# Conv tower: the low fp16 parts of every layer made by GpSimd alone, DVE keeping the high parts and the statistics

## The chip, the core and the metric

The kernel runs on one core of one Trainium2 chip. The metric is the device time of one execution in microseconds. The core has TensorE (PE; matmuls, weight loads shown apart as PEld), VectorE (DVE), ScalarE (ACT), GpSimd (POOL) and SyncE (SP, which issues transfers); each works through its own instructions in order and waits on semaphores for the others.

## What is computed

An audio tower in fp32: six convolution layers, one attention layer with 12 heads, one layer of 8 experts with top-1 routing, for a batch of 4 sequences of 120,000 samples. The change concerns the convolutions only:

```python
CONV_LAYERS = [(128, 10, 5), (128, 3, 2), (128, 3, 2), (128, 3, 2), (128, 3, 2), (128, 2, 2)]
NUM_GROUPS = 32

def _block(x, cw, cb, gw, gb, stride):
    y = lax.conv_general_dilated(x, cw, (stride,), 'VALID', dimension_numbers=('NCH', 'OIH', 'NCH'))
    y = y + cb[None, :, None]
    B, C, T = y.shape
    yg = y.reshape(B, NUM_GROUPS, C // NUM_GROUPS * T)
    mu = yg.mean(axis=-1, keepdims=True)
    var = yg.var(axis=-1, keepdims=True)
    yn = ((yg - mu) * lax.rsqrt(var + EPS)).reshape(B, C, T)
    yn = yn * gw[None, :, None] + gb[None, :, None]
    return jax.nn.gelu(yn)
...
h = tower(x)
h = h + attention(layernorm(h))
h = h + experts(layernorm(h))
```

The group normalisation of a layer needs the mean and variance over the whole sequence of the layer's output, so a layer's activations can't be finished before its last convolution is.

## The kernel before

**Two fp16 parts.** TensorE multiplies in fp16, and each fp32 activation is kept as two fp16 parts: the high part is the value cast to fp16, the low part is the value less the high part. A convolution is summed from three products per tap: high weights and low weights with the high part, high weights with the low part. In a group of up to 9 matmuls (3 taps) the 6 with the high part come first, and the 3 with the low part wait for it. All parts lie in one large SBUF tile, `arena`, whose rows have 126 columns; 8 rows are 1008 elements per partition.

**A pass of the tower.** The tower runs once per sequence, four passes in all, and nothing of a pass overlaps the next pass's tower. In a pass:

1. Layer 0's output is made in 24 pieces of 8 rows (`conv0` jobs, three per block j). TensorE makes a piece in PSUM, ScalarE normalises it into one of 4 staging buffers (line 991), DVE casts it to the high part (1178), and GpSimd or DVE makes the low part (794 or 1181). A staging buffer is written again when high and low part of the piece four earlier are done. Layer 1's convolutions, 96 rows in jobs of two cuts of 4 rows, are interleaved: a cut reads rows from the three pieces of a block, so it waits for the parts of a block's last piece (2, 5, 8, ...). Their outputs go through ScalarE (972) to fp32 rows, and DVE takes their statistics (`bn_stats`, line 1315, 1311 and 1312).
2. When the last statistics are in, a short chain (aggregate 1093, TensorE's group average 1703, GpSimd's power 769, DVE 1116) gives scale and bias. ScalarE normalises layer 1's 96 rows in 13 chunks of 5, 4, ten times 8, and 7 rows (903), DVE casts each chunk, one of the two engines makes the low part, and TensorE begins layer 2's 48 rows as the chunks come in. After the last cast DVE copies one row of the high and one of the low part to the end of the buffer, the halo (1171, 1172), which the last convolution job of the next layer waits for. Only then, in DVE's order, come the statistics of layer 2's rows.
3. The same for layer 2 (7 chunks), layer 3 (4 chunks) and layer 4 (2 chunks, no halo). Layer 5's output goes into the attention.

**Who makes a low part** is decided by `low_engine`: of layer 0, DVE makes every third piece (2, 5, 8, ...) and GpSimd the others; of layers 1 to 4, DVE the even chunks (0, 2, 4, ...) and GpSimd the odd ones. DVE makes its low part right behind the cast of the same chunk. GpSimd makes each when `hi_done` says that its cast is done (`low_parts`, line 794), in the chunks' order. TensorE and ScalarE wait for the low parts by the two counters `lo_dve` and `lo_pool`. Attention, experts and the work between passes use neither of the two lines.

Of the kernel before, what the change touches and what calls it, by code (L numbers as in the profile page):

```python
# [50 lines left out]
ACT_ENGINE, DVE_ENGINE = "act", "dve"  # L51
# [92 lines left out]
SETUP, TOWER, PAIR, LAST_PAIR, POST, MOE = range(6)  # L144
# [47 lines left out]


def low_engine(layer, piece):
    if layer == 0:
        return DVE_ENGINE if piece % 3 == 2 else "pool"
    return "pool" if piece % 2 else DVE_ENGINE

# [9 lines left out]
    "affine_ready": (1, CONV_LAYERS - 1, 0, 0, 1),  # L210
    "norm_done": (0, sum(len(c) for c in NORM_CHUNKS.values()), 0, 0, 0),
    "hi_done": (0, len(SPLITS), 0, 0, 0),
    "lo_dve": (0, sum(low_engine(*u) == DVE_ENGINE for u in SPLITS), 0, 0, 0),
    "lo_pool": (0, sum(low_engine(*u) == "pool" for u in SPLITS), 0, 0, 0),
    "halo_done": (0, 4, 0, 0, 0),
    "xn_ready": (0, 1, 0, 0, 1),
# [103 lines left out]
def audio_tower(nc, ins, out):  # L320
# [8 lines left out]
    with ctx:  # L329
# [543 lines left out]
        def _(act):  # L873
# [87 lines left out]
            with act.Fori(0, BATCH) as b:  # L961
                layer = 0
                for g, n, kind, args in jobs_of(TOWER):
                    if kind == "conv":
                        if args[0] > 1 and args[1] == 0:
                            normalise(args[0] - 1, b)
                        layer, r, cut = args
                        wait(act, "ps_full", TOWER, n + 1, b)
                        rows = cut[0]
                        dst = ys[layer][:, r * PITCH:(r + sum(cut)) * PITCH]  # L970
                        src = slot(g).rearrange("p (k n) -> p k n", k=2)[:, 0:len(cut), 0:rows * PITCH]
                        a.activation(dst.rearrange("p (k n) -> p k n", k=len(cut)), src, ACT.Identity,  # L972
                                     scale=1.0 / WSCALE).then_inc(S["act_freed"], 1)
                    elif kind == "conv0":
                        j, i = args
                        if args == (0, 0):
                            wait(act, "affine_ready", TOWER, 0, b)

                            wait(act, "scratch_stored", TOWER, 0, b)
                        wait(act, "ps_full", TOWER, n + 1, b)  # L980
                        piece = 3 * j + i
                        if piece >= STAGES:

                            had_it = (0, piece - STAGES)
                            wait(act, "hi_done", TOWER, SPLITS.index(had_it) + 1, b)
                            if low_engine(*had_it) == DVE_ENGINE:
                                wait(act, "lo_dve", TOWER, lows(DVE_ENGINE, had_it), b)
                            else:
                                wait(act, "lo_pool", TOWER, lows("pool", had_it), b)
                        src = slot(g).rearrange("p (m n) -> p m n", m=2)[:, :, 0:4 * PITCH]  # L990
                        a.activation(stage[:, piece % STAGES, :].rearrange("p (m n) -> p m n", m=2), src,  # L991
                                     ACT.Gelu_apprx_tanh,
                                     bias=affine[:, 1:2], scale=affine[:, 0:1]).then_inc(S["act_freed"], 1)
                    elif kind in ("q", "k", "v", "s"):
                        attention_job(TOWER, g, n, kind, args, b)
                    else:
                        assert kind == "xtr"
                        if layer == 5:
                            normalise(5, b)
                            layer = None  # L1000
                        wait(act, "ps_full", TOWER, n + 1, b)
                        a.activation(xt_parts[:, args[0], :], bank(g, 0).bitcast(fp16)[:, 0:TOK], ACT.Copy
                                     ).then_inc(S["act_freed"], 1)
                with act.Fori(0, PAIRS - 1) as pr:
                    for g, n, kind, args in jobs_of(PAIR):
                        attention_job(PAIR, g, n, kind, args, b, pr)
                for g, n, kind, args in jobs_of(LAST_PAIR):
                    attention_job(LAST_PAIR, g, n, kind, args, b)
                for g, n, kind, args in jobs_of(POST):
                    wait(act, "ps_full", POST, n + 1, b)  # L1010
                    a.activation(xnt1[0:D1, 0:TOK], slot(g)[0:D1, 0:TOK], ACT.Copy).then_inc(S["act_freed"], 1)
# [22 lines left out]
        def _(dve):  # L1034
# [139 lines left out]
            def split(unit, b):  # L1174

                src, high, low = split_views(*unit)
                n = SPLITS.index(unit) + 1
                v.tensor_copy(high, src).then_inc(S["hi_done"], 1)  # L1178
                if low_engine(*unit) == DVE_ENGINE:
                    dve.wait_ge(S["hi_done"], at("hi_done", TOWER, n, b))  # L1180
                    v.tensor_tensor(low, src, high, ALU.subtract).then_inc(S["lo_dve"], 1)  # L1181

            def wait_split(unit, b):
                wait(dve, "hi_done", TOWER, SPLITS.index(unit) + 1, b)
                for engine, name in ((DVE_ENGINE, "lo_dve"), ("pool", "lo_pool")):
                    if lows(engine, unit):
                        wait(dve, name, TOWER, lows(engine, unit), b)

            def attention_job(phase, n, kind, args, b, pr=None):
                g = slot_of(phase, n)  # L1190
# [283 lines left out]
        def _(pe):  # L1474
# [213 lines left out]
            with pe.Fori(0, BATCH) as b:  # L1688
                for n, (kind, args, who) in enumerate(JOBS[TOWER]):
# [11 lines left out]
                    elif kind == "group":  # L1701
                        wait(pe, "channel_stats", TOWER, args[0], b)
                        last = t.matmul(bank(g, 0)[:, 0:2], group_avg[:, :], ms[:, :], start=True, stop=True)
                    elif kind == "conv":
                        layer, r, cut = args
                        taps = 2 if layer == 5 else 3
                        parts = [a.rearrange("p (r c) -> p r c", c=PITCH) for a in hs[layer - 1]]

                        terms = [(tap, w, 0) for tap in range(taps) for w in (0, 1)]
                        terms += [(tap, 0, 1) for tap in range(taps)]  # L1710
                        for k, c in enumerate(cut):
                            need = 2 * (r + c) - 2 + taps - 1
                            if need >= ROWS[layer - 1]:
                                wait(pe, "halo_done", TOWER, layer, b)
                                need = ROWS[layer - 1] - 1
                            unit = split_unit_of(layer - 1, need)
                            wait(pe, "hi_done", TOWER, SPLITS.index(unit) + 1, b)
                            for tap, w, x in terms:
                                if (tap, w, x) == (0, 0, 1):
                                    for engine, name in ((DVE_ENGINE, "lo_dve"), ("pool", "lo_pool")):  # L1720
                                        wait(pe, name, TOWER, lows(engine, unit), b)
                                f = 2 * r + tap
                                last = t.matmul(bank(g, k)[:, 0:c * PITCH].rearrange("p (r c) -> p r c", c=PITCH),  # L1723
                                                cwt[layer][:, w, tap, :], parts[x][:, f:f + 2 * c - 1:2, :],
                                                start=(tap, w, x) == terms[0], stop=(tap, w, x) == terms[-1])
                            r += c
                    elif kind == "embed":
                        if args[0] == 0:
                            wait(pe, "norm_done", TOWER, COUNTS["norm_done"][1], b)
                        tiles = range(4) if args[0] == 0 else range(4, TT)  # L1730
                        for q, i in enumerate(tiles):
                            m = tile_rows(i)
                            last = t.matmul(bank(g, q // 2)[0:m, (q % 2) * D:(q % 2 + 1) * D],
                                            h5t[:, 128 * i:128 * i + m], pwt[:, :], start=True, stop=True)
                    else:
                        assert kind == "xtr"
                        if args[0] == 0:
                            wait(pe, "xn_ready", TOWER, 1, b)
                        for i in range(TT):
                            m = tile_rows(i)  # L1740
                            last = t.transpose(bank(g, 0).bitcast(fp16)[:, 128 * i:128 * i + m],
                                               xn_parts[0:m, i, args[0], :], ident_h[0:m, 0:m])
# [142 lines left out]
```

## Time and profile before

| | |
|---|---|
| median of 3 runs | 1911.61 us |
| lowest, highest | 1901.88, 1912.4 us |
| span of the profiled execution | 1912.2 us |
| busy share of the span: PE, DVE, ACT, POOL | 80%, 58%, 40%, 31% |
| passes of the tower, from the first cast of layer 0 to the last cast of layer 4 | 39.80 to 184.15, 440.53 to 586.29, 842.56 to 988.86, 1245.38 to 1391.67 us |

The busy shares are averages over the tower, the attention and the experts. Durations count from an instruction's start, which can lie before the moment at which it gets what it needs, so an instruction can be long because it is held. Successive instructions of one engine overlap a little at their ends: two casts of 0.67 us take 1.27 in a row.

### The profile page before, as it was taken

The numbers are of one execution on the slowest core, as the hardware profiler recorded it, in microseconds if no ns is written. First come the engines' busy times: TensorE is split into PE (matmuls) and PEld (weight loads), VectorE is DVE, ScalarE is ACT, GpSimd is POOL, SyncE is SP. The second block draws the span as 40 slices with busy tenths as digits, with TensorE's granted clock in tenths as the row PEclk, the third lists the DMA queues.
The fourth block names the chain that finished last, engine by engine and source line by source line (L and its number), as shares of the span: only waits on it lengthen the run. The fifth ranks groups of instructions, "written<-read, shape, count | busy, mean of one in ns | idle before, by whom it ended". The sixth has DMA issues, their size and how long they took to land.

```text
span 1912.2 us, 33119 instructions
## 1 busy us (share of the span) xinstructions
PE 1539.1 (80%) x10013; PEld 1020.7 (53%) x10014; DVE 1109.6 (58%) x2520; ACT 757.7 (40%) x1456; POOL 600.9 (31%) x502
## 2 busy tenths in 40 slices
PE   6975699998865899889657999898659999339997
PEld 4332476783333666763334666833336667327775
DVE  5986455568884555669864555598845555302221
ACT  2643344425542444425533444165324443002221
POOL 3732133305431333236322333064213331421111
PEclk6987799998986999979877999989869999659999
DMA  4200121210000221110001222100014332621110
GB/s 125 80 1 1 34 57 41 56 34 12 1 1 1 65 56 41 33 36 1 1 1 40 53 48 51 30 11 1 1 28 105 89 73 66 199 69 46 48 47 20
DMA packets 105852, 81.31 MB, mean 43 GB/s; under 512 B 57842, under 2 KB 96267, under 8 KB 105747
## 3 DMA queue, kind: packets, MB, share of 16 engines
q1 hardware_dynamic: 99988, 70.65, 14.6%
q0 software_dynamic: 5760, 9.36, 1.6%
q8 instruction: 54, 0.88, 0.2%
q14 instruction: 50, 0.41, 0.1%
HBM read 34.66 MB, written 18.38 MB: 28 GB/s over the span
## 4 chain that ended last, share of the span: by engine, by line
issue 40%; PE 35%; POOL 15%; DVE 5%; SPq 2%; DMA 2%; ACT 1%; POOLq 0%; DVEq 0%; ACTq 0%
POOL arena L794 10%; PE ps L1676 8%; PE ps L1618 6%; PE ps L1650 4%; PE ps L1662 3%; PE ps L1830 3%; PE ps L1625 2%; PE ps L1810 2%; PE ps L1811 2%; DVE arena L1212 2%; DVE smax L1203 2%; POOL slot_scratch L848 1%; PE ps L1818 1%; SPq L552 1%; PE ps L1831 1%
## 5 line engine op out<-in xcount | busy, mean ns | idle before, releaser
L1723 PE MATMUL ps<-arena,cwt 128*128 128x504 f16 (+2 forms) x1776 | 409.8, 392 | 85.3 <-DVE arena L1178 59.9
L1723 PEld LDWEIGHTS ps<-arena,cwt 128*128 128x128 f16 x1776 | 179.4, 105 | 305.9 <-DVE arena L1178 66.2
L794 POOL TENSOR_TENSOR arena<-arena 128x1008 f16<-128x1008 f32 (+2 forms) x112 | 255.6, 2292 | 196.6 <-DVE arena L1178 196.6
L1676 PE MATMUL ps<-arena 128*128 128x64 f32 (+2 forms) x2016 | 261.2, 270 | 22.9 <-DVE arena L1212 22.9
L1203 DVE TENSOR_REDUCE smax<-ps 128x1 f32<-128x128 f32 (+5 forms) x288 | 177.2, 615 | 172.1 <-PE ps L1653 172.1
L1676 PEld LDWEIGHTS ps<-arena 128*128 128x128 f32 (+2 forms) x2016 | 242.3, 189 | 44.2 <-issue 28.5
L1212 DVE COPY arena<-ps 128x512 f32<-128x512 f32 (+4 forms) x288 | 157.4, 546 | 83.7 <-PE ps L1662 83.6
L1181 DVE TENSOR_TENSOR arena<-arena 128x1008 f16<-128x1008 f32 (+2 forms) x88 | 200.3, 2276 | 3.0
L917 ACT ACTIVATE arena<-ps,nmax 128x128 f32<-128x128 f32 (+5 forms) x288 | 180.6, 627 | 53.5 <-DVE nmax L1204 50.7
L1178 DVE CAST arena<-arena 128x1008 f16<-128x1008 f32 (+4 forms) x200 | 176.9, 914 | 32.6 <-ACT arena L903 16.1
L1650 PE MATMUL ps<-arena 128*128 128x512 f16 (+6 forms) x780 | 163.7, 313 | 28.9 <-ACT arena L957 16.3
L1662 PE MATMUL ps<-ident,arena 128*128 128x128 f32 (+2 forms) x1008 | 168.0, 284 | 12.1 <-ACT arena L957 5.7
L972 ACT ACTIVATE arena<-ps 128x1008 f32<-128x1008 f32 (+1 forms) x112 | 96.1, 865 | 186.3 <-PE ps L1723 186.3
L957 ACT ACTIVATE arena<-ps,rinv 128x64 f32<-128x64 f32 (+1 forms) x288 | 90.9, 315 | 162.3 <-PE ps L1676 153.1
L903 ACT ACTIVATE arena<-arena,affine 128x1008 f32<-128x1008 f32 (+5 forms) x108 | 113.2, 1125 | 95.3 <-DVE affine L1116 95.3
L1662 PEld LDWEIGHTS ps<-ident,arena 128*128 128x128 f32 (+2 forms) x1008 | 108.1, 144 | 55.3 <-ACT arena L957 39.1
L778 POOL TENSOR_TENSOR arena<-arena,ones_col 128x750 f16<-128x750 f32 x40 | 57.4, 1434 | 212.7 <-ACT arena L934 212.7
L991 ACT ACTIVATE arena<-ps,affine 128x1008 f32<-128x1008 f32 x96 | 109.6, 1191 | 29.1 <-POOL arena L794 28.6
L1315 DVE BATCH_NORM_STATS2 bn<-arena 128x6 f32<-128x500 f32 (+1 forms) x180 | 102.8, 624 | 26.9 <-ACT arena L972 26.9
L758 POOL TENSOR_TENSOR w_parts<-wqkv,wscale_col 128x384 f16<-128x384 f32 x25 | 20.7, 827 | 303.8 <-PE ps L1625 281.4
L1650 PEld LDWEIGHTS ps<-arena 128*128 128x128 f16 (+2 forms) x780 | 77.6, 118 | 58.1 <-ACT arena L957 21.7
L1017 ACT ACTIVATE arena<-ps 128x768 f32<-128x768 f32 x31 | 25.2, 812 | 198.4 <-PE ps L1811 198.4
(249 smaller groups left out, 2181.1 us busy)
## 6 DMA issues: line engine op xcount, KB each, us to landing
arena<-arena SPq DMA_DIRECT2D x96, 187.5 KB, 2.9
arena<-arena SPq DMA_DIRECT2D x96, 93.8 KB, 2.5
slot_scratch<-empty_slot SPq DMA_DIRECT2D x1, 5775.0 KB, 18.6
arena<-in_L_ffn_w SPq DMA_DIRECT2D x8, 576.0 KB
arena<-in_L_ffn_w SPq DMA_DIRECT2D x8, 384.0 KB
arena<-slot_scratch SPq DMA_DIRECT2D x31, 96.5 KB, 1.9
arena<-slot_scratch SPq DMA_DIRECT2D x31, 96.0 KB, 2.0
xa<-in_x POOLq DMA_DIRECT2D x5, 468.8 KB, 4.2
```

The costliest lines, as they stand in the source:

```text
L794: g.tensor_tensor(low, src, high, ALU.subtract).then_inc(S["lo_pool"], 1)
L903: a.activation(dst, src, ACT.Gelu_apprx_tanh, bias=affine[:, 1:2], scale=affine[:, 0:1]).then_inc(S["norm_done"], 1)
L917: a.activation(prob[k % PROBS][0:m, 0:128 * i + m], slot(g)[0:m, 0:128 * i + m], ACT.Exp, bias=nmax[0:m, k_:k_ + 1], scale=SCALE, accum_ou ...
L1178: v.tensor_copy(high, src).then_inc(S["hi_done"], 1)
L1181: v.tensor_tensor(low, src, high, ALU.subtract).then_inc(S["lo_dve"], 1)
L1203: step(v.reduce_max(smax[0:m, k_:k_ + 1], slot(g)[0:m, 0:128 * i + m], AX.X))
L1212: v.tensor_copy(probt[k % 2][:, 0:w, 0:m], src[:, 0:w, 0:m]).then_inc(S["dve_freed"], 1)
L1618: last = t.matmul(bank(g, k)[:, 0:TOK // 2], weights, x, start=m == 0, stop=m == len(terms) - 1)
L1650: last = t.matmul(slot(g)[0:m, lo:hi], q, keys[:, lo:hi], start=a == 0, stop=a == len(terms) - 1 and not diagonal)
L1662: last = t.transpose(slot(g)[0:kk, 128 * c:128 * c + m], prob[k % PROBS][0:m, 128 * c:128 * c + kk], ident[0:m, 0:m])
L1676: last = t.matmul(slot(g)[0:m, Z_AT:Z_AT + DH], probt[k % 2][0:kk, c, 0:m], vt[0:kk, c, DH * hh:DH * hh + DH], start=c == 0, stop=c == i)
L1723: last = t.matmul(bank(g, k)[:, 0:c * PITCH].rearrange("p (r c) -> p r c", c=PITCH), cwt[layer][:, w, tap, :], parts[x][:, f:f + 2 * c - 1 ...
```

## The change

`low_engine` answers "pool" for every layer and piece. DVE's subtract, the wait in front of it and the counter `lo_dve` go; TensorE, ScalarE and DVE wait for `lo_pool` alone, counted to the unit in question. Nothing else is changed: the same 200 low parts are made, all by GpSimd.

```diff
 def low_engine(layer, piece):
-    if layer == 0:
-        return DVE_ENGINE if piece % 3 == 2 else "pool"
-    return "pool" if piece % 2 else DVE_ENGINE
+    return "pool"
...
-    "lo_dve": (0, sum(low_engine(*u) == DVE_ENGINE for u in SPLITS), 0, 0, 0),
...
                             wait(act, "hi_done", TOWER, SPLITS.index(had_it) + 1, b)
-                            if low_engine(*had_it) == DVE_ENGINE:
-                                wait(act, "lo_dve", TOWER, lows(DVE_ENGINE, had_it), b)
-                            else:
-                                wait(act, "lo_pool", TOWER, lows("pool", had_it), b)
+                            wait(act, "lo_pool", TOWER, lows("pool", had_it), b)
...
                 src, high, low = split_views(*unit)
-                n = SPLITS.index(unit) + 1
                 v.tensor_copy(high, src).then_inc(S["hi_done"], 1)
-                if low_engine(*unit) == DVE_ENGINE:
-                    dve.wait_ge(S["hi_done"], at("hi_done", TOWER, n, b))
-                    v.tensor_tensor(low, src, high, ALU.subtract).then_inc(S["lo_dve"], 1)
...
                                 if (tap, w, x) == (0, 0, 1):
-                                    for engine, name in ((DVE_ENGINE, "lo_dve"), ("pool", "lo_pool")):
-                                        wait(pe, name, TOWER, lows(engine, unit), b)
+                                    wait(pe, "lo_pool", TOWER, lows("pool", unit), b)
```

In the rows below, `arena` is the tile that holds all parts, and the rows with line 529 (before) or 526 (after) are the engine's preparation of a wait. The casts are at 1178 before and 1171 after, the low parts at 1181 (DVE) and 794 (GpSimd) before and 791 after, the halo copies at 1171 and 1172 before and 1165 and 1166 after, the statistics at 1315 before and 1303 after.

On DVE, a block of three pieces of layer 0, before:

```order
L1178 CAST arena<-arena 128x2x4x126
L529 REGISTER_ALU
L1178 CAST arena<-arena 128x2x4x126
L529 REGISTER_ALU
L1178 CAST arena<-arena 128x2x4x126
L1180 REGISTER_ALU
L1181 TENSOR_TENSOR arena<-arena 128x2x4x126
L529 REGISTER_ALU
L1315 BN_STATS bn<-arena 128x6 x2
```

and after:

```order
L1171 CAST arena<-arena 128x2x4x126
L526 REGISTER_ALU
L1171 CAST arena<-arena 128x2x4x126
L526 REGISTER_ALU
L1171 CAST arena<-arena 128x2x4x126
L526 REGISTER_ALU
L1303 BN_STATS bn<-arena 128x6 x2
```

The third piece's subtract is gone, and the statistics follow the casts.

On DVE, the end of layer 1's splits, before:

```order
L1178 CAST arena<-arena 128x1008
L529 REGISTER_ALU
L1178 CAST arena<-arena 128x882
L1180 REGISTER_ALU
L1181 TENSOR_TENSOR arena<-arena 128x882
L529 ISA
L529 REGISTER_ALU
L1171 COPY arena<-arena 128x126
L1172 COPY arena<-arena 128x126
L529 REGISTER_ALU
L1315 BN_STATS bn<-arena 128x6 x2
```

and after:

```order
L1171 CAST arena<-arena 128x1008
L526 REGISTER_ALU
L1171 CAST arena<-arena 128x882
L526 REGISTER_ALU
L1165 COPY arena<-arena 128x126
L1166 COPY arena<-arena 128x126
L526 REGISTER_ALU
L1303 BN_STATS bn<-arena 128x6 x2
```

The halo copies stood behind DVE's own last low part and now stand right behind the last cast.

On GpSimd, the start of layer 1's low parts behind the power that ends layer 1's statistics, before:

```order
L769 TENSOR_TENSOR tmp<-tmp,neg_half 128x1
L529 REGISTER_ALU
L794 TENSOR_TENSOR arena<-arena 128x504
L529 REGISTER_ALU
L794 TENSOR_TENSOR arena<-arena 128x1008
```

and after:

```order
L766 TENSOR_TENSOR tmp<-tmp,neg_half 128x1
L526 REGISTER_ALU
L791 TENSOR_TENSOR arena<-arena 128x630
L526 REGISTER_ALU
L791 TENSOR_TENSOR arena<-arena 128x504
L526 REGISTER_ALU
L791 TENSOR_TENSOR arena<-arena 128x1008
```

Of layer 1 GpSimd makes 13 low parts where it made 6; the first and the last one, of 630 and 882 elements, were DVE's.

## Rows read from the trace of the kernel before

**Rows 1.** The page's groups: line, engine, shapes, count | busy us, mean ns | idle before.

```profile
L794 POOL TENSOR_TENSOR arena<-arena 128x1008 f16<-128x1008 f32 (+2 forms) x112 | 255.6, 2292 | 196.6 <-DVE arena L1178 196.6
...
L1181 DVE TENSOR_TENSOR arena<-arena 128x1008 f16<-128x1008 f32 (+2 forms) x88 | 200.3, 2276 | 3.0
```

**Rows 2.** Stretch of stage 1: length, then PE, PEld, DVE, ACT, POOL busy, PEclk.

```profile
69.50:85.00 15.50, 14.33 (x68) 6.16 (x67) 15.31 (x15) 9.68 (x10) 10.77 (x4) 1.00 0.00 0
```

**Rows 3.** Timeline (start, us) of DVE, POOL; last two: chain of waits, 36 to 200.

```profile
85.45 1.85 DVE L1178 CAST arena<-arena 128x1008 f16<-128x1008 f32 x3
87.33 2.91 DVE L1181 TENSOR_TENSOR arena<-arena 128x1008 f16<-128x1008 f32 x1
...
86.19 5.94 POOL L794 TENSOR_TENSOR arena<-arena 128x1008 f16<-128x1008 f32 x2 [4.06 <-DVE arena L1178]
...
89.14 2.99 POOL arena L794
...
95.11 2.47 POOL arena L794
```

**Rows 4.** Timeline of POOL: the first low part of pass one.

```profile
40.58 2.02 POOL L794 TENSOR_TENSOR arena<-arena 128x1008 f16<-128x1008 f32 x1 [2.91 <-DVE arena L1178]
```

**Rows 5.** Timeline: first cast and last 30 matmuls of stage 1, passes one and three.

```profile
39.80 0.69 DVE L1178 CAST arena<-arena 128x1008 f16<-128x1008 f32 x1 [2.72 <-ACT arena L991]
...
98.78 6.55 PE L1723 MATMUL ps<-arena,cwt 128*128 128x504 f16 x30 [0.67 <-DVE arena L1181]
...
842.56 1.42 DVE L1178 CAST arena<-arena 128x1008 f16<-128x1008 f32 x2 [2.85 <-ACT arena L991]
...
902.83 6.55 PE L1723 MATMUL ps<-arena,cwt 128*128 128x504 f16 x30 [0.67 <-DVE arena L1181]
```

**Rows 6.** Timeline of DVE, POOL and PE in stage 2 of pass one.

```profile
111.64 0.49 DVE L1178 CAST arena<-arena 128x630 f16<-128x630 f32 x1 [0.98 <-ACT arena L903]
...
116.16 1.27 DVE L1178 CAST arena<-arena 128x1008 f16<-128x1008 f32 x2
...
136.37 0.18 DVE L1171 COPY arena<-arena 128x126 f16<-128x126 f16 x1
136.47 0.18 DVE L1172 COPY arena<-arena 128x126 f16<-128x126 f16 x1
136.57 6.53 DVE L1315 BATCH_NORM_STATS2 bn<-arena 128x6 f32<-128x250 f32 x12
...
143.78 0.53 DVE L1093 BATCH_NORM_AGGREGATE mv<-bn 128x2 f32<-128x84 f32 x1
...
113.39 1.07 POOL L794 TENSOR_TENSOR arena<-arena 128x504 f16<-128x504 f32 x1 [3.43 <-DVE arena L1178]
116.92 2.34 POOL L794 TENSOR_TENSOR arena<-arena 128x1008 f16<-128x1008 f32 x1 [2.46 <-DVE arena L1178]
...
136.78 2.08 PE L1723 MATMUL ps<-arena,cwt 128*128 128x504 f16 x9 [0.40 <-DVE arena L1172]
```

**Rows 7.** Timeline of DVE in stage 3 of pass one: first cast, aggregate.

```profile
148.10 0.49 DVE L1178 CAST arena<-arena 128x630 f16<-128x630 f32 x1 [0.98 <-ACT arena L903]
...
164.54 0.37 DVE L1093 BATCH_NORM_AGGREGATE mv<-bn 128x2 f32<-128x48 f32 x1
```

**Rows 8.** Timeline of DVE and PE in stage 4 of pass one.

```profile
168.49 0.49 DVE L1178 CAST arena<-arena 128x630 f16<-128x630 f32 x1 [0.98 <-ACT arena L903]
...
178.18 0.28 DVE L1093 BATCH_NORM_AGGREGATE mv<-bn 128x2 f32<-128x30 f32 x1
...
169.04 7.70 PE L1723 MATMUL ps<-arena,cwt 128*128 128x252 f16 x36 [3.24 <-DVE arena L1178]
```

**Rows 9.** Timeline of DVE, POOL and PE in stage 5 of pass one.

```profile
182.15 0.55 DVE L1178 CAST arena<-arena 128x756 f16<-128x756 f32 x1 [1.08 <-ACT arena L903]
...
184.23 1.62 POOL L794 TENSOR_TENSOR arena<-arena 128x756 f16<-128x756 f32 x1 [3.61 <-DVE arena L1178]
...
182.76 3.83 PE L1723 MATMUL ps<-arena,cwt 128*128 128x378 f16 x12 [3.41 <-DVE arena L1178]
```

More of the change, by code:

```diff
@@ L1176, in split @@
                 src, high, low = split_views(*unit)
-                n = SPLITS.index(unit) + 1
                 v.tensor_copy(high, src).then_inc(S["hi_done"], 1)
-                if low_engine(*unit) == DVE_ENGINE:
-                    dve.wait_ge(S["hi_done"], at("hi_done", TOWER, n, b))
-                    v.tensor_tensor(low, src, high, ALU.subtract).then_inc(S["lo_dve"], 1)
             def wait_split(unit, b):
                 wait(dve, "hi_done", TOWER, SPLITS.index(unit) + 1, b)
-                for engine, name in ((DVE_ENGINE, "lo_dve"), ("pool", "lo_pool")):
-                    if lows(engine, unit):
-                        wait(dve, name, TOWER, lows(engine, unit), b)
+                wait(dve, "lo_pool", TOWER, lows("pool", unit), b)
             def attention_job(phase, n, kind, args, b, pr=None):
@@ L1719, in _ @@
                                 if (tap, w, x) == (0, 0, 1):
-                                    for engine, name in ((DVE_ENGINE, "lo_dve"), ("pool", "lo_pool")):
-                                        wait(pe, name, TOWER, lows(engine, unit), b)
+                                    wait(pe, "lo_pool", TOWER, lows("pool", unit), b)
                                 f = 2 * r + tap
```

## The prediction, made before the change was run

> **What bounds the kernel now.** I read the page's groups first. The low parts are made by GpSimd (line 794) 112 times and by DVE (line 1181) 88 times, 2.3 us each [rows 1]: 22 and 28 in each of the four passes of the tower. All of them lie in the tower, so the rest of the program (attention, experts) keeps its time, and the question is how five stages per pass move: stage 1 (conv0 pieces and layer 1's convolutions), then the splits of layers 1, 2, 3 and 4 with the convolution behind each. Next the busy times by stretch: in 15.5 us of stage 1 TensorE is busy 14.33, DVE 15.31, GpSimd 10.77 [rows 2]. DVE and TensorE are both nearly full there. Last the instructions in order of time, where DVE's fullness turns out to be partly waiting.
>
> **Two engines that exclude each other.** DVE's subtract for a piece is issued at 87.33 and lasts 2.91; GpSimd's two instructions begin at 86.19 and the second at 89.14, for 2.99 [rows 3]. DVE's casts end at 87.30, so the first low runs 87.30 to about 89.18, then DVE's subtract does its work (90.24 is its end, 1.06 after), then the second low (1.89, to 92.13). Each runs while the other stands still. A cast between two lows shows the same: with one in between, a low takes 2.47 [rows 3], without one 2.02 [rows 4]. So when GpSimd has the next low queued, the two alternate: low, cast, low, cast. An 8-row low from stage 2 on starts at 116.92 while casts end at 117.43 and is done at 119.26 [rows 6]: 1.83 after them. With a 0.59 cast in front (two casts take 1.27 including the last one's tail [rows 6]) that is 2.42 per piece.
>
> The Trainium skill ("SBUF — State Buffer", Who interferes with whom) states that DVE and GpSimd share one port pair under an exclusive lock, that a two-input DVE instruction or a 2-port copy or cast takes it, and that issue order decides who blocks. By that, the trace agrees. By that page the two halves never ran in parallel, and what speaks for moving them (DVE has less to do) is worth only what DVE does without the lock, the statistics.
>
> **What the change does, by price.** DVE's low costs 1.06 of exclusive time per 1008 elements, GpSimd's 1.83 to 1.89. Each of 88 moved lows therefore adds about 0.8 of exclusive time, 17 us a pass, unless gaps take it. How much reaches the end is read stage by stage. In all of them l and c are the low and the cast of a chunk.
>
> *The halo copies.* Per layer, DVE copies one row of the high and one of the low part (126 fp16) after the last cast. Before, DVE's own low or an idle GpSimd stood ahead of them, so they were never held (0.18 each [rows 6]). Now GpSimd has a low running and one queued. If they need the same exclusion, the first copy waits for l11 and the second for the last low, l12, and all statistics of the layer are queued behind them on DVE. No row shows a copy issued into a running low. The nearest: the two copies start 0.10 apart, and the statistics 0.10 behind them [rows 6]; DVE's exclusive subtract moves 1008 elements in 1.06, which for 126 is 0.13 without any fixed part. So the copies run faster than a one-stream instruction, as the casts do (1008 in 0.59), and casts are held. Bounds of their wait: zero, and the rest of two lows. I take the held case.
>
> The Trainium skill ("VectorE: DVE Perf Modes", Mode 4×_2P) states that four elements per cycle need both ports. By that page the held case would hold, and a pass costs 12 us rather than 4.
>
> *Stage 1.* To l1 nothing changes (45.6). l2 was DVE's, now GpSimd ends it at 48.1, and TensorE's first low matmul waits 1.3 longer. GpSimd then goes l3 50.5, l4 53.0; halo copy, l5 55.1, second copy; statistics; casts 6, 7 (both before l6), l6 59.4, l7 61.9, l8 64.3. From there TensorE needs 21 matmuls (4.5), conv0 (1.3), 18 (3.9), conv0, 15 (3.2), 14.3 in all, before it wants l14; GpSimd needs four lows at 2.46 and two at 2.02 plus 0.7 to restart after it has run dry behind the statistics: 14.6. So l14 at 78.9, and in the next six the casts fall one later, 15.5: l20 94.4, and three at up to 2.46: l23 101.4. That is 61.6 after the first cast. Before, TensorE took up the last 30 matmuls at 98.78, 59.0 after the first cast in pass one, and 60.3 in pass three (842.56 to 902.83) [rows 5]. Added: 2.6 and 1.3. I take 1.8 for each pass. GpSimd thus stays about as fast as the old pair, which took 15.45 for six: the ramp costs it.
>
> *Stage 2 (layer 1's splits, 13 chunks).* First cast ends at 112.1. l0 (630 elements, 1.35 by the 504 at 1.07 [rows 6]) ends 113.5; c1 and c2 slip in; l1 115.4; c3, l2 117.85; then 2.42 each: l11 139.6; copy; l12 (882 elements, 1.65) 141.35; copy 141.45. Statistics took 136.57 to 143.78, 7.21, without a wait [rows 6]: now 141.5 to 148.7. Their inputs are there: TensorE's last nine matmuls, behind the halo, take 2.08 to 143.6, and DVE reaches the last two after 147.9. Added 4.9.
>
> *Stage 3 (7 chunks).* The same steps from the first cast (148.10): l1 at 3.76, l2 6.2, l5 13.45, copy, l6 15.2, copy 15.3; statistics 3.75: 19.1. Before 164.54, i.e. 16.44 [rows 7]. Added 2.65.
>
> *Stage 4 (4 chunks).* l2 at 6.2, copy, l3 8.0, copy 8.1. Here statistics wait for TensorE: its last job starts only behind the halo, nine matmuls, to 10.15, and the aggregate comes 1.44 after TensorE's end (176.74 to 178.18 [rows 8]): 11.6 against 9.69. Added 1.9.
>
> *Stage 5 (2 chunks, no halo).* Both lows are GpSimd's in a row: the first blocks c1 from 182.75 to 184.37, l1 goes 184.95 to 186.57 against 185.85 (184.23 and 1.62), and TensorE ends 0.74 behind it as before [rows 9]. Added 0.7.
>
> The sum: 1.8 + 4.9 + 2.65 + 1.9 + 0.7 = 11.95 per pass, 47.8 for four. On the profiled execution's own span, 1912.2, that is 1960; the median of the runs shown is 1911.6, so the two can be taken as one. What is removed (one wait on DVE in each split, one wait name on TensorE) costs nothing visible: no row shows idle time at it.
>
> **Rivals.** *The copies are not held.* What speaks for it: every copy in the trace took 0.18. Then DVE starts statistics after its last cast: stage 2 at 137.9 (+1.35), stage 3 held by TensorE's last low (+1.2), stage 4 +0.5, stage 5 +0.7, stage 1, where the two copies no longer push the lows back, +0.5. 4.25 a pass, 17 in all: 1929. Against it: their pace.
> *Faster.* One mechanism: a cast between two queued lows adds nothing to GpSimd's pace, so that a low costs 2.02. Then stage 1 is left to TensorE (14.33 per six for 15.45, 4.5 a pass), stage 2's twelve units of eight rows end when they did (24.2 for 24.3) and its statistics begin a little earlier (1): -22, 1890. It decides where low and cast together fall below 2.03 in stage 2 (24.3 over 12); 2.47 and 2.42 speak against it.
> *Slower still.* Stage 1's four staging buffers: ScalarE may write piece k+4 only after l_k. If this closes a loop (low, activation, cast, low) whenever GpSimd runs dry, each six cost 17.5: 8 more per pass, 1992. For it: cast and activation of one piece lie between lows four apart, on two engines that have other work in between; against it: GpSimd runs dry only once in six in my steps.
>
> **How the numbers follow.** Copies held, as summed: 0.63. Not held: 0.17. Staging loop: 0.14. Faster: 0.06. Predicted 1960. Stage 1 is the softest term (between 0 and 4 a pass), which gives 1945 to 1975 for the likeliest case; the range takes in most of the first rival and half of the way to the loop: 1925 to 1985. A measurement here can tell about 1% (19 us). Faster 0.06; within 1% 0.12 (most of the 1929 case and little else); slower 0.82.
>
> **What the changed profile would show.** Right: line 791 200 times, with 2.4 to 2.5 each in stage 2, back to back; casts of about 2.4 between them; the second halo copy lasting some 1.7 instead of 0.18, and statistics of layer 2 starting some 5 later after the first cast; attention and experts as before. Wrong: halo copies at 0.18 while line 791 runs (then 1929); lows at 2.02 with casts between; ScalarE's conv0 activations waiting over 3 us for line 791; or stage 1 shorter than 59 from first cast to the last 30 matmuls.

## The result: about 20 us slower, and the profile after

The changed kernel takes 1930.3 us (median of four runs, 1929.5 to 1943.7) against 1910.2 us for the kernel before beside it (1901.9 to 1912.4). The ratio is 1.0133 with a 95% interval of 1.0093 to 1.0173: slower by 1.3%, some 20 us, where 48 were forecast. From the page of the kernel after: the span, the busy times, and the groups of the low parts and of the casts (line, engine, shapes, count | busy us, mean ns | idle before).

```profile
span 1927.8 us, 32831 instructions
...
PE 1536.8 (80%) x10013; PEld 1008.0 (52%) x10014; DVE 1097.7 (57%) x2432; ACT 757.4 (39%) x1456; POOL 776.5 (40%) x590
...
L791 POOL TENSOR_TENSOR arena<-arena 128x1008 f16<-128x1008 f32 (+4 forms) x200 | 430.8, 2181 | 69.8 <-DVE arena L1171 69.8
L1171 DVE CAST arena<-arena 128x1008 f16<-128x1008 f32 (+4 forms) x200 | 327.5, 1681 | 38.2 <-ACT arena L900 21.6
```

GpSimd makes all 200 low parts at 2.2 us each, beside the 112 of [rows 1]. DVE lost 88 subtracts of 200.3 us together and is busy only 12 us less than before: its casts, 0.6 us of work for eight rows, now take 1.7 on average, because they wait.

The time by stage, worked out from the timeline of DVE: from the first cast of a stage to the aggregate that ends it (us). The last column is the growth of a whole pass, from its first cast to its last aggregate.

| pass | stage 1 before, after | stage 2 | stage 3 | stage 4 | stage 5 | pass |
|---|---|---|---|---|---|---|
| 1 | 66.97, 71.12 | 32.14, 34.55 | 16.44, 17.30 | 9.69, 10.49 | 6.42, 6.99 | +8.5 |
| 2 | 67.93, 68.25 | 32.15, 34.57 | 16.44, 17.30 | 10.30, 10.48 | 6.55, 6.88 | +4.1 |
| 3 | 68.27, 68.34 | 32.14, 34.55 | 16.45, 17.30 | 10.50, 10.47 | 6.54, 6.88 | +3.6 |
| 4 | 68.29, 68.31 | 32.15, 34.56 | 16.44, 17.30 | 10.47, 10.48 | 6.55, 6.88 | +3.5 |

The last column adds up to 19.7 us. The first expert transfer starts 19.4 later (1673.02 after, 1653.59 before), so all of it is in the tower. From there to the end the two profiled executions differ by 3.8 us the other way (the span grows by 15.6 only), with the same code on both sides. In the profiled executions here that last stretch lies between 253 and 259 us with the same code, so the stage times are the finer measure.

**Stage 2, the alternation.** DVE (first six rows), GpSimd, and TensorE in stage 2 of pass one of the kernel after:

```profile
115.05 0.49 DVE L1171 CAST arena<-arena 128x630 f16<-128x630 f32 x1 [0.98 <-ACT arena L900]
...
117.98 22.51 DVE L1171 CAST arena<-arena 128x1008 f16<-128x1008 f32 x10 [0.20 <-ACT arena L900]
140.41 1.96 DVE L1165 COPY arena<-arena 128x126 f16<-128x126 f16 x1
142.29 0.18 DVE L1166 COPY arena<-arena 128x126 f16<-128x126 f16 x1
142.39 6.53 DVE L1303 BATCH_NORM_STATS2 bn<-arena 128x6 f32<-128x250 f32 x12
149.60 0.53 DVE L1087 BATCH_NORM_AGGREGATE mv<-bn 128x2 f32<-128x84 f32 x1
...
117.27 26.80 POOL L791 TENSOR_TENSOR arena<-arena 128x504 f16<-128x504 f32 x12 [0.36 <-DVE arena L1171]
...
140.07 2.09 PE L1710 MATMUL ps<-arena,cwt 128*128 128x504 f16 x9 [0.28 <-POOL arena L791]
142.37 2.73 PE L1710 MATMUL ps<-arena,cwt 128*128 128x504 f16 x12 [0.21 <-POOL arena L791]
```

The chain of waits in the same stretch (start, us, what):

```profile
137.61 0.66 POOL arena L791
...
139.97 0.59 POOL arena L791
...
142.28 1.79 POOL arena L791
```

GpSimd runs 12 lows without a gap, one per 2.36 us (137.61 to 139.97), and ten casts that are 0.6 each of work fill 22.5. TensorE has its nine matmuls done in 2.09 and stands until the next low part. The first halo copy waits 1.96 us for a low. The second, one line on, takes 0.18, although GpSimd has its last low still to make (142.28 to 144.07): it slips in first, and the statistics start at 142.39 while that low runs, at their full speed (6.53 for twelve, as in [rows 6]). Stage 2 is 2.4 us longer than [rows 6] have it.

**Stage 1.** DVE's two halo copies in passes one and two, then GpSimd over six pieces in pass one, then TensorE where it takes up the pieces behind low part 8, in passes one and two:

```profile
39.51 0.69 DVE L1171 CAST arena<-arena 128x1008 f16<-128x1008 f32 x1 [2.71 <-ACT arena L985]
50.62 2.02 DVE L1165 COPY arena<-arena 128x126 f16<-128x126 f16 x1
52.56 2.06 DVE L1166 COPY arena<-arena 128x126 f16<-128x126 f16 x1
...
459.90 2.01 DVE L1165 COPY arena<-arena 128x126 f16<-128x126 f16 x1
461.83 0.18 DVE L1166 COPY arena<-arena 128x126 f16<-128x126 f16 x1
...
75.74 11.67 POOL L791 TENSOR_TENSOR arena<-arena 128x1008 f16<-128x1008 f32 x5 [0.62 <-DVE arena L1171]
...
90.92 11.66 POOL L791 TENSOR_TENSOR arena<-arena 128x1008 f16<-128x1008 f32 x5 [0.62 <-DVE arena L1171]
...
63.77 6.32 PE L1710 MATMUL ps<-arena,cwt 128*128 128x504 f16 x21 [1.95 <-POOL arena L791]
...
472.04 4.64 PE L1710 MATMUL ps<-arena,cwt 128*128 128x504 f16 x21 [0.89 <-POOL arena L791]
```

Six pieces take GpSimd 15.18 (75.74 to 90.92), where the pair of engines took 15.45 before: in its steady part stage 1 loses nothing. Pass one loses 1.2 us of ramp to a second copy that is held, and TensorE stands 1.95 us for low 8. What follows that wait is a lower granted clock. The stretches (length, then PE, PEld, DVE, ACT, POOL busy, PEclk) after that wait, in the kernel after:

```profile
62.00:66.00 4.00, 2.23 (x8) 0.94 (x9) 4.00 (x2) 1.59 (x2) 4.00 (x2) 0.84 0.00 0
66.00:70.00 4.00, 4.00 (x15) 1.57 (x14) 1.84 (x3) 0.00 (x0) 4.00 (x3) 0.73 0.00 0
```

and the stretch 60 to 68 in the kernel before:

```profile
60.00:68.00 8.00, 7.35 (x36) 3.05 (x34) 7.84 (x6) 4.13 (x5) 6.05 (x3) 1.00 0.01 4
```

A mean of 0.73 says that part of this stretch ran at the lower level (1.2 GHz) and part at 2.4 GHz. The 21 matmuls take 6.32 us instead of the 4.64 of pass two, 1.7 more. Together, 1.2 and 1.7 account for the 2.8 by which stage 1 of pass one now lasts longer than in the other passes. The rest of its 4.15 lies in the kernel before, whose own pass one was 1.0 to 1.3 shorter than its other passes. Passes two to four grow by 0.0 to 0.3 only.

**Stages 3 and 4.** DVE in stage 3 (first two rows) and stage 4 of pass one of the kernel after:

```profile
153.92 0.49 DVE L1171 CAST arena<-arena 128x630 f16<-128x630 f32 x1 [0.98 <-ACT arena L900]
171.22 0.37 DVE L1087 BATCH_NORM_AGGREGATE mv<-bn 128x2 f32<-128x48 f32 x1
175.17 0.49 DVE L1171 CAST arena<-arena 128x630 f16<-128x630 f32 x1 [0.98 <-ACT arena L900]
...
179.39 2.08 DVE L1165 COPY arena<-arena 128x126 f16<-128x126 f16 x1
181.39 0.18 DVE L1166 COPY arena<-arena 128x126 f16<-128x126 f16 x1
...
185.66 0.29 DVE L1087 BATCH_NORM_AGGREGATE mv<-bn 128x2 f32<-128x30 f32 x1
```

The same pattern: first copy held, second not, 17.30 and 10.49 us against the 16.44 and 9.69 of [rows 7, 8]. Of all 16 pairs of copies in the kernel after, the first is held every time and the second once:

```profile
L1165 DVE COPY arena<-arena x16: 1955/1986/2087, 50.6 to 1398.4; 128x126 f16<-128x126 f16 x16
...
L1166 DVE COPY arena<-arena x16: 182/184/2062, 52.6 to 1400.4; 128x126 f16<-128x126 f16 x16
```

These are the views of the two lines: duration in ns, least/median/most.

### The profile page after: what moved, and what is told of

Same layout as the page of the kernel before. It is cut to its first block, busy times and chain, and to the rows that moved or that the text cites. A ratio compares the mean times of both kernels' runs of the same rounds, so it can differ in the third digit from the quotient of the medians.

```text
span 1927.8 us, 32831 instructions
## 1 busy us (share of the span) xinstructions
PE 1536.8 (80%) x10013; PEld 1008.0 (52%) x10014; DVE 1097.7 (57%) x2432; ACT 757.4 (39%) x1456; POOL 776.5 (40%) x590
## 4 chain that ended last, share of the span: by engine, by line
issue 40%; PE 35%; POOL 14%; DVE 5%; SPq 2%; DMA 2%; ACT 1%; POOLq 0%; DVEq 0%; ACTq 0%
POOL arena L791 10%; PE ps L1664 8%; PE ps L1606 5%; PE ps L1638 4%; PE ps L1650 3%; PE ps L1817 3%; PE ps L1613 2%; PE ps L1797 2%; PE ps L1798 2%; DVE arena L1200 2%; DVE smax L1191 2%; POOL slot_scratch L845 1%; PE ps L1805 1%; SPq L549 1%; PE ps L1818 1%
## 5 line engine op out<-in xcount | busy, mean ns | idle before, releaser
L1710 PE MATMUL ps<-arena,cwt 128*128 128x504 f16 (+2 forms) x1776 | 417.3, 391 | 100.4 <-DVE arena L1171 59.9
L791 POOL TENSOR_TENSOR arena<-arena 128x1008 f16<-128x1008 f32 (+4 forms) x200 | 430.8, 2181 | 69.8 <-DVE arena L1171 69.8
L1171 DVE CAST arena<-arena 128x1008 f16<-128x1008 f32 (+4 forms) x200 | 327.5, 1681 | 38.2 <-ACT arena L900 21.6
L1710 PEld LDWEIGHTS ps<-arena,cwt 128*128 128x128 f16 x1776 | 172.9, 104 | 336.1 <-POOL arena L791 94.3
L766 POOL TENSOR_TENSOR tmp<-tmp,neg_half 128x1 f32<-128x1 f32 x25 | 13.9, 555 | 186.3 <-DVE tmp L1100 186.3
```

Of the source, the lines that this page charges most:

```text
L791: g.tensor_tensor(low, src, high, ALU.subtract).then_inc(S["lo_pool"], 1)
```

## The experiments

The theory of the first three: GpSimd's low part and DVE's two-port and two-input work exclude each other, so what counts is the exclusive time of each piece, and GpSimd's low is the dearer one (1.85 against 1.06); the first halo copy is held behind it. The rival: it is an engine that is full of work of its own.

**All low parts on DVE.** The opposite of the change, from the kernel before. The wait for a counter that no longer counts goes too.

```diff
 def low_engine(layer, piece):
-    if layer == 0:
-        return DVE_ENGINE if piece % 3 == 2 else "pool"
-    return "pool" if piece % 2 else DVE_ENGINE
+    return DVE_ENGINE
...
-                                        wait(pe, name, TOWER, lows(engine, unit), b)
+                                        if lows(engine, unit):
+                                            wait(pe, name, TOWER, lows(engine, unit), b)
```

> The opposite of the change: every low part on DVE, right behind its cast, none on GpSimd. Theory (the two engines exclude each other, and a low costs 1.06 us of exclusive time on DVE against 1.83 to 1.89 on GpSimd): a piece costs 1.65 of DVE, so stage 1 is left to TensorE (14.3 per six pieces for 15.45, 4 us a pass), stage 2 from first cast to aggregate falls from 32.1 to about 28.4, stages 3 and 5 by 0.5 and 0.7. 9 us a pass: about 1875. Rival (a DVE low costs the 2.28 that the page gives as its mean, and DVE, busy 15.3 of 15.5 us in stage 1, is the bound): six pieces then take 21 us instead of 15.45, 22 us a pass, about 2000.

Measured: 1873.7 us (1873.1 to 1876.7), 0.9804 of before (0.9782 to 0.9826), 38 us faster than before and 57 faster than the change. DVE in a block of stage 1 and at the two ends of stage 2 of pass one, and the stretch 60 to 80:

```profile
66.45 0.67 DVE L1176 CAST arena<-arena 128x1008 f16<-128x1008 f32 x1
67.16 1.21 DVE L1179 TENSOR_TENSOR arena<-arena 128x1008 f16<-128x1008 f32 x1
68.28 0.68 DVE L1176 CAST arena<-arena 128x1008 f16<-128x1008 f32 x1
...
105.74 0.49 DVE L1176 CAST arena<-arena 128x630 f16<-128x630 f32 x1 [0.98 <-ACT arena L901]
...
135.51 0.53 DVE L1091 BATCH_NORM_AGGREGATE mv<-bn 128x2 f32<-128x84 f32 x1
...
60.00:80.00 20.00, 20.00 (x95) 8.71 (x94) 19.73 (x26) 12.60 (x13) 0.00 (x0) 1.00 0.01 1
```

Cast and subtract of a piece take 1.84 together (66.45 to 68.28), about as long as GpSimd's low alone. Stage 2 is 29.77, stage 1 61.80 in every pass; TensorE is busy all of the 20 us, so there stage 1 is now TensorE's, with DVE (19.73) close behind. DVE makes all 200 subtracts, 112 more than before, and is busy 1079 us, less than the 1110 of before and the 1098 of the change. So in the kernel before DVE wasn't full of work: it was full of waiting.

The total came out as expected (1875), but partly because misses cancelled. Stage 2 was expected at 28.4, with 1.65 for a piece that takes 1.84. Stage 5 gained nothing where 0.7 was expected, and stage 4 of pass one became 1.0 longer (10.69). Stage 1 gained 5.2 to 6.5 a pass where 4 was expected.

**The halo copies on ScalarE.** From the kernel after; nothing on DVE is held after its last cast.

```diff
+            def act_halo(layer, b):
+                unit = (layer, 0)
+                wait(act, "hi_done", TOWER, SPLITS.index(unit) + 1, b)
+                wait(act, "lo_pool", TOWER, lows("pool", unit), b)
+                r = ROWS[layer] * PITCH
+                high, low = hs[layer]
+                a.activation(high[:, r:r + PITCH], high[:, 1:1 + PITCH], ACT.Copy)
+                a.activation(low[:, r:r + PITCH], low[:, 1:1 + PITCH], ACT.Copy).then_inc(S["halo_done"], 1)
...
-                                wait_split((layer, 0), b)
-                                halo(layer, b)
```

> The changed kernel with the halo copies made by ScalarE behind its normalisation, and none on DVE. Theory (the first copy, held by GpSimd's low for 1.96 us, holds back the statistics behind it): stage 2 from first cast to aggregate falls from 34.6 to 32.6, stages 3 and 4, where TensorE's last job is waited for, by less than 0.3, stage 1 of pass one by 1 to 2. About 10 us less than the changed kernel, 1920. Rival (only GpSimd's slower pace counts, and TensorE would end as late anyway): stage 2 stays within 0.4 of 34.6, and the time within 3 us of the changed kernel's.

Measured: 1917.1 us (1915.8 to 1922.8, ten runs), 1.0038 of before (1.0026 to 1.0050). DVE in stage 2 of pass one:

```profile
112.10 0.49 DVE L1185 CAST arena<-arena 128x630 f16<-128x630 f32 x1 [0.98 <-ACT arena L910]
...
115.04 22.51 DVE L1185 CAST arena<-arena 128x1008 f16<-128x1008 f32 x10 [0.20 <-ACT arena L910]
137.47 6.53 DVE L1311 BATCH_NORM_STATS2 bn<-arena 128x6 f32<-128x250 f32 x12
...
144.69 0.53 DVE L1101 BATCH_NORM_AGGREGATE mv<-bn 128x2 f32<-128x84 f32 x1
```

The casts are as slow as in the change, the statistics follow the last one, and stage 2 takes 32.59, 1.96 less than the 34.55 of the change: the first copy's wait. So of the 2.4 us of stage 2, 2.0 are the held copy. Only 0.45 are left of the slower alternation, because DVE, which no longer makes the last low, begins the statistics before it is there. Stages 3 to 5 gained nothing (17.30, 10.5 to 11.0, 7.2): stage 3's last twelve matmuls wait for GpSimd's low parts in both kernels and end 1.44 before the aggregate, so TensorE ends that stage and not DVE. Stage 1 of pass one fell from 71.12 to 68.39, more than the 1 to 2 us expected: TensorE waits 0.90 for low 8, and the granted clock is at 1.00 from 62 to 70. The passes of this execution are together 11.4 longer than before's, its first expert transfer comes 8.5 later, and the medians differ by 5.5: the rest lies in stretches between and behind the passes whose code is the same, and it shows how far one execution can be trusted outside the stages.

**Only layer 0, and only layers 1 to 4, on GpSimd.** From the kernel before, half of the change each, both with the same guard on TensorE's wait as in the first experiment:

```diff
     if layer == 0:
-        return DVE_ENGINE if piece % 3 == 2 else "pool"
+        return "pool"
     return "pool" if piece % 2 else DVE_ENGINE
```

> Only layer 0's low parts moved to GpSimd, layers 1 to 4 as before. By the comparison of the two traces the change's loss in stage 1 is 4 us in pass one and under 0.5 in the others: stage 1 should read 71.1, 68.3, 68.3, 68.3 from first cast to aggregate, the later stages as before (32.1, 16.4), and the time be 4 us above before. Rival (stage 1 costs in every pass what pass one shows): 16 us above.

```diff
-    return "pool" if piece % 2 else DVE_ENGINE
+    return "pool"
```

> Only the low parts of layers 1 to 4 moved to GpSimd, layer 0 as before. If the parts add up: stage 1 67.0 to 68.3 as before, stage 2 34.6, stage 3 17.3, stage 4 10.5, stage 5 6.9, about 3.7 us a pass, 15 above before. Rival (the stages only shift waits, and stage 1's release hides them): within 4 us of before.

Measured: layer 0 alone 1914.1 us (1912.0 to 1917.5, ten runs), 1.0015 (1.0002 to 1.0028); layers 1 to 4 alone 1926.2 us (1924.1 to 1927.0), 1.0077 (1.0053 to 1.0100). The two add up to 17 us of the 20. Stage 1 moved all the way to GpSimd costs between 0.4 and 0.8 in passes two to four and 2.2 in pass one (69.20); there the second copy was not held and the stretch in question kept its clock:

```profile
62.00:70.00 8.00, 7.12 (x34) 2.95 (x33) 6.36 (x5) 3.28 (x4) 8.00 (x4) 1.00 0.00 1
```

So the expectation of 71.1 in pass one was missed: that loss is not a fixed part of moving layer 0. Layers 1 to 4 came out as expected in total (15 us), but with stages 3 and 4 off in three places. Stage 3 took 18.49 in passes one and two and 17.30 in the others, and stage 4 11.78 in pass two; in just these three places of the twelve the second copy was held. DVE at the end of stage 3's splits, pass one, of the kernel with layers 1 to 4 moved:

```profile
160.28 1.96 DVE L1171 COPY arena<-arena 128x126 f16<-128x126 f16 x1
162.15 1.78 DVE L1172 COPY arena<-arena 128x126 f16<-128x126 f16 x1
```

With the code of the change from the first cast of a layer on, the second copy was held here as forecast, and stage 3 cost 2.05 more than before where the forecast was 2.65. Whether the second copy gets in ahead of GpSimd's next low is thus not fixed by the code.

**Eight halo copies for two.** From the kernel after, with a tile `halo_pad` that nobody reads. The question is whether any copy behind the first gets in, or only one that is early enough.

```diff
                 v.tensor_copy(high[:, r:r + PITCH], high[:, 1:1 + PITCH])
+                for i in range(6):
+                    v.tensor_copy(halo_pad[:, i, :], high[:, 1:1 + PITCH])
                 v.tensor_copy(low[:, r:r + PITCH], low[:, 1:1 + PITCH]).then_inc(S["halo_done"], 1)
```

> The changed kernel with six more copies of the high halo row (into a spare tile) between the first and the last copy: eight in a row, 0.10 us each. Theory (each short copy takes the pair anew, and GpSimd's queued low gets in as soon as it asks, about 0.1 us after its predecessor's end): one of the copies behind the first is held for the whole last low, in every layer, so stage 2 from first cast to aggregate grows from 34.6 to about 36.9 (1.7 for the low and 0.6 for the copies). Rival (copies in a row keep the pair once they have it): only the first is held, and stage 2 grows by 0.6, to 35.2.

Measured in a single run: 1967.6 us beside 1912.9 before. DVE in stage 2 of pass one, the six copies as one row and then the first two of them by themselves:

```profile
141.50 1.96 DVE L1166 COPY arena<-arena 128x126 f16<-128x126 f16 x1
143.37 2.25 DVE L1168 COPY halo_pad<-arena 128x126 f16<-128x126 f16 x6
...
143.37 0.18 DVE L1168 COPY halo_pad<-arena 128x126 f16<-128x126 f16 x1
143.47 1.74 DVE L1168 COPY halo_pad<-arena 128x126 f16<-128x126 f16 x1
```

Six copies take 2.25 instead of 0.6: one of them waits 1.65, the length of the last low of 882 elements (as forecast for l12), and the other five are free. Stage 2 is 36.72. The same holds in all sixteen groups of six (2.25 to 2.57 each). The trace also says which copy is held. The one right behind the first, where the change has its second, gets in (0.18) in 15 of the 16 groups, and the one after it is held (1.74 to 2.02); in the remaining group, in stage 1 of pass three, the one right behind the first is held (2.06). So one short copy can get in between two lows, but two in a row never did, and the second copy of the change escapes only by being the very next.

The clock shows in this run too. Stage 1 takes 72.0 to 72.3 in all four passes, and in each TensorE waits 2.83 to 3.15 for low 8 and then needs 6.13 to 6.32 for its 21 matmuls, with a mean granted clock of 0.72 to 0.74 over them (0.72 in pass one of the change, 1.00 in its pass two).

**GpSimd working beside DVE for nobody.** From the kernel with all lows on DVE: GpSimd subtracts one broadcast column from itself into an unread tile, once per piece, after the piece's cast.

```diff
+                            wait(pool, "hi_done", TOWER, SPLITS.index(unit) + 1, b)
+                            g.tensor_tensor(beside[:, 0:cols], ones_col[:, :].to_broadcast([128, cols]), ones_col[:, :].to_broadcast([128, cols]), ALU.subtract).then_inc(S["pool_busy"], 1)
```

> All low parts on DVE as in the kernel with none on GpSimd, and beside them GpSimd makes, for each chunk, a subtract of the same length from a broadcast constant into a spare tile that nobody reads; nothing but GpSimd waits for it. Theory (the engines exclude each other whatever they touch): each chunk costs cast, DVE's subtract and GpSimd's instruction in turn, so in stage 2 the casts and subtracts are held up to 1.9 us, the first cast to aggregate grows from 29.8 to 40 or more, and the time goes to 1950 or more. Rival (they only get in each other's way where they touch the same data or wait by semaphore): 1874, stage 2 at 29.8.

Measured in a single run: 2155.5 us, 282 more than without it. DVE and GpSimd in stage 1 of pass one:

```profile
77.53 1.21 DVE L1188 TENSOR_TENSOR arena<-arena 128x1008 f16<-128x1008 f32 x1
78.65 2.35 DVE L1185 CAST arena<-arena 128x1008 f16<-128x1008 f32 x1
81.04 1.21 DVE L1188 TENSOR_TENSOR arena<-arena 128x1008 f16<-128x1008 f32 x1
82.16 2.42 DVE L1322 BATCH_NORM_STATS2 bn<-arena 128x6 f32<-128x500 f32 x4
...
77.57 2.89 POOL L795 TENSOR_TENSOR beside<-ones_col 128x1008 f16<-128x1008 f32 x1 [0.62 <-DVE arena L1185]
81.08 2.89 POOL L795 TENSOR_TENSOR beside<-ones_col 128x1008 f16<-128x1008 f32 x1 [0.62 <-DVE arena L1185]
```

This is the plainest proof of the exclusion: none of DVE's work depends on that tile, and a piece takes 3.51 instead of 1.84, 1.67 more, close to one GpSimd subtract. At 77.53 DVE's subtract goes first and GpSimd's waits (2.89 from 77.57), then GpSimd runs and DVE's cast waits (2.35). The statistics go on at 0.6 each while GpSimd's second subtract runs (82.16 for four), so they don't take part.

The Trainium skill ("SBUF — State Buffer", Who interferes with whom) states such a lock between a GpSimd instruction and DVE's two-input or 2-port work. This run agrees, with 1.67 us per piece beside it.

**All on DVE, and the halo copies on ScalarE.** Both edits of above at once, to see whether the faster version still gains from the second.

> All low parts on DVE and the halo copies on ScalarE. With GpSimd out of the tower the copies cost DVE 0.2 us a layer, and none is held: by the theory the time is that of the kernel with all low parts on DVE (1874) within 3 us, stage 2 at 29.6 to 29.8. Rival (the copies cost by their place in DVE's order, not by being held): stage 2 falls by 2 as it did in the changed kernel, 1865.

Measured: 1871.9 us (1870.8 to 1874.9), 0.9791 of before (0.9775 to 0.9808), not to be told from 0.9804. Stage 2 is 29.55, 0.2 less. Once no low of GpSimd's is about, the copies cost their 0.2 and no more.

## Why the prediction was right in direction and too high in size

The time of 1930.3 lies in the stated range (1925 to 1985), but below the 1945 to 1975 given for the likeliest case. It is in the range by the room that was left for the first rival and not by the sum.

- **Two engines that exclude each other: right.** It was read from before's rows [rows 3] and carried the direction. All on DVE gained 38 us, and GpSimd's unread work cost 282.
- **The alternation low, cast: right.** 2.42 per piece was forecast and 2.36 measured in stage 2; in stage 1 15.5 per six, 15.18 measured.
- **The first halo copy held: right.** The trace of before showed none held; the argument from its pace (0.10 apart for 126 elements, [rows 6]) gave it. It was held 1.96 to 2.09 in all 16 places.
- **The second halo copy held, "and the second for the last low, l12": this step failed.** It was held in one place of 16. I had taken for granted that GpSimd, with its next low queued, gets its turn after every DVE instruction, as it does between casts. But the second copy follows the first at once (142.29 to 142.47) and mostly is through before GpSimd has the ports again: its last low, 1.65 of work, is counted from 142.28 and ends 1.79 later, which leaves about 0.14 (an estimate) for the copies. The run with eight copies agrees: the copy 0.10 behind the second one was held in 15 of 16 places. Where a copy behind the first was held, the cost came nearer to the forecast, though still below it: 2.05 in stage 3 for 2.65 (layers 1 to 4 moved), and with eight copies, of which the third was held, 4.0 in stage 2 for 4.9 (4.58 less the 0.6 of the added copies). By these places the failed step is worth 1.65 in stage 2 (the wait), 1.2 in stage 3 (18.49 for 17.30) and 1.3 in stage 4 (11.78 for 10.48).
- **Stage 2, +4.9 forecast, +2.4 measured.** 1.65 from the second copy, 0.6 from the pace (ten chunks at 2.36 for 2.42), the rest in the ramp.
- **Stage 3, +2.65 forecast, +0.86 measured**: the second copy again; with it held, +2.05.
- **Stage 4, +1.9 forecast, +0.8 in pass one and -0.03 to +0.18 in the others: two errors.** The second copy was one. The other is mine: I set the forecast 11.6 against 9.69 [rows 8], which is pass one alone; before took 10.30 to 10.50 in the other three. TensorE's 36 matmuls took 7.70 in pass one and 8.3 to 8.5 in the others; the mean granted clock over them was 0.77 in pass one, 0.71 in pass two and 0.69 in pass three. I had looked at pass three for stage 1, and not here, and multiplied by four.
- **Stage 5, +0.7 forecast, +0.57 and 0.33 three times**: the mechanism as told, its size from one pass again.
- **Stage 1, +1.8 forecast, +4.15, +0.32, +0.07 and +0.02 measured, 1.1 on average.** In pass one the steps hold up to low 8: 24.5 after the first cast was forecast and 24.26 measured, with both copies held. The slower matmuls at the lower clock behind the wait, 1.7, were not in the sum, and pass one's measured growth is also taken from a pass of before that was 1.0 to 1.3 shorter than the others. In the later passes the second copy was free, low 8 came 1.2 earlier, and the six pieces at 15.18 made up the rest.
- **The staging loop, 0.14: did not occur.** Six pieces took 15.18, not 17.5. **Faster, 0.06: did not occur,** by the pace of 2.36.
- **"Copies not held", 1929: its number is the nearest, its mechanism is not what happened.** It had stage 2 at +1.35 and stage 3 at +1.2 with neither copy held, and the first always was. The kernel without held copies, the one with ScalarE's, took 1917.

By terms per pass, forecast and measured mean over four passes: 1.8 and 1.1, 4.9 and 2.4, 2.65 and 0.9, 1.9 and 0.2, 0.7 and 0.4; sums 11.95 and 5.0. Of the 6.9 between them the second copy has 4.15 in stages 2 to 4, stage 4's one pass taken for four 0.55 (before's mean is 10.24), stage 2's pace 0.6, stages 1 and 5 the 1.0 by which their terms were too large; 0.6 remain spread over the ramps.

What stays open is what decides the tie of the second copy: the same code holds it in one pass and not in the next. The experiments show how often and at what price: right behind the held first copy it was held in 5 of 48 places (1 of 16 in the change, none of 4 with layer 0 moved, 3 of 12 with layers 1 to 4 moved, 1 of 16 with eight copies). They don't show why in those. The lower granted clock goes with the length of TensorE's wait for low 8: it came all five times behind a wait of 1.95 to 3.15 us (pass one of the change, all four with eight copies), and was absent all eleven times behind one of 0.88 to 0.91 (passes two to four of the change, all four passes with layer 0 alone moved and with the copies on ScalarE). No run changed that wait and nothing else, so that the wait is the cause is argued and not shown.

## What to carry to other kernels

Before work is moved from DVE to GpSimd, look for rows of both engines in which each lasts longer while the other is at work: if they exclude each other, what decides is the sum of the two engines' exclusive times, so here the engine that needs less for a piece did best with all of it, and a lower busy share of DVE was no gain. A DVE subtract costs 1.06 and a GpSimd one 1.85, and the order of the totals is that of the pace per chunk: 1.84 us (all DVE, 1874), 2.03 (shared, 1911), 2.36 (all GpSimd, 1930). And where a term is multiplied by the number of passes, it is to be read in each of them.

## What the runs showed of the hardware

- A short DVE copy (126 fp16 elements, 0.10 us) right behind another that was held mostly gets in ahead of a waiting GpSimd instruction: it was held in 5 of 48 places. The copy after it didn't get in: it was held in 15 of 15 places. Behind a cast of 0.6 GpSimd's next low came first in the whole alternation of stage 2.
- The statistics ran at 0.6 us per 500 columns while GpSimd worked, in every kernel: of DVE's work in the tower they are what can lie beside GpSimd's.
- GpSimd's subtract of one broadcast fp32 column from itself lasts about as long as that of an fp16 from an fp32 tensor (1.8 us for 1008 elements, 2.89 less the 1.1 of its wait, beside 1.83 to 1.89): reading two full tensors cost it nothing that shows.
- Busy time counts waiting: DVE with all 200 subtracts is busy 1079 us, DVE with none of them 1098.
